# Expert rows scattered straight from the mixer, and expert results added to the token rows in memory by accumulating indirect DMAs

## The reference

```
x = x + xattn(layernorm(x), ctx)          # 16 heads; q and the output projection with int8 fake quantisation
x = x + scan(layernorm(x))                # 16 states per channel, 64 steps, sequential in the tokens
x = x + ffn(layernorm(x))

ffn: probs = softmax(x @ gate_w.T);  scores, idx = top_k(probs, 8)        # 64 experts
     pos = the place of a (token, expert) pair among those of its expert, in token order
     valid = pos < C,  C = 2 * 2048 * 8 / 64 = 512
     xbuf[e, pos] = x[token]  (pairs beyond C are dropped)
     y = (silu(xbuf @ w_gate.T) * (xbuf @ w_up.T)) @ w_down.T
     out[token] += y[e, pos] * score * valid
```

## Time and profile before

| | us |
|---|---|
| median of 3 runs | 2778.35 (2775.64 to 2782.33) |
| the profiled execution | 2786.16 |
| its span in the trace | 2784.4 |
| TensorE busy in the span | 2299.9 (83%) |
| VectorE, ScalarE, GpSimd busy | 1790.8, 1417.8, 976.9 |
| memory traffic | 163.44 MB read, 40.30 MB written |

### The profile page before, as it was taken

The page is one execution under the profiler, slowest core; times in us unless marked ns, Lnnn a source line. Parts: engine busy times, 40 slices in busy tenths (PEclk is TensorE's granted clock), DMA queues, the critical chain, the costliest instruction groups (busy, mean ns, idle before and its releaser), DMA issues. The chain is left out here.

```text
span 2784.4 us, 58439 instructions
## 1 busy us (share of the span) xinstructions
PE 2299.9 (83%) x22156; PEld 1557.6 (56%) x22156; DVE 1790.8 (64%) x3152; ACT 1417.8 (51%) x2948; POOL 976.9 (35%) x1037
## 2 busy tenths in 40 slices
PE   5998999989898989899999999898982399999300
PEld 3665665656565656566565656565651276666200
DVE  4457776877776776777676777777776355454333
ACT  1556565655565565656565656656572144444100
POOL 1112223232323222322322231322223476776576
PEclk9999999999999999999999999999996699999655
DMA  2011101010111111121101010111000388788543
GB/s 78 25 51 54 66 25 63 33 56 33 55 33 56 33 55 38 50 75 37 63 33 55 33 56 33 55 33 56 31 33 36 76 228 223 212 219 210 142 122 111
DMA packets 109499, 207.09 MB, mean 74 GB/s; under 512 B 17136, under 2 KB 86384, under 8 KB 107216
## 3 DMA queue, kind: packets, MB, share of 16 engines
q1 hardware_dynamic: 86688, 153.24, 15.7%
q0 software_dynamic: 22576, 50.56, 8.5%
HBM read 163.44 MB, written 40.30 MB: 73 GB/s over the span
## 5 line engine op out<-in xcount | busy, mean ns | idle before, releaser
L772 ACT ACTIVATE sb_probsT<-W 128x512 f32<-128x512 f32 (+1 forms) x1024 | 472.4, 511 | 420.2 <-PE W L610 418.0
L782 ACT ACTIVATE sb_probs<-S,sb_negmax 128x1604 f32<-128x1604 f32 x256 | 409.1, 1598 | 250.0 <-DVE sb_negmax L939 249.3
L610 PE MATMUL W<-sb_ident,sb_probs 128*128 128x128 f32 (+1 forms) x3328 | 484.8, 284 | 50.5 <-DVE sb_z L1013 50.2
L939 DVE TENSOR_REDUCE sb_negmax<-S 128x1 f32<-128x1604 f32 x256 | 465.7, 1819 | 10.8 <-PE S L600 10.7
L610 PEld LDWEIGHTS W<-sb_ident,sb_probs 128*128 128x128 f32 (+1 forms) x3328 | 357.5, 141 | 167.1 <-issue 104.4
L572 PE MATMUL W<-sb_ctx,sb_wkv_in 128*32 128x401 f32 x4096 | 417.3, 527 | 32.8 <-DVE sb_V L934 27.7
L582 PE MATMUL W<-sb_wkv_in,sb_ctx 128*128 128x256 f32 (+1 forms) x1664 | 422.0, 397 | 21.8 <-DVE sb_K_lo L924 18.9
L625 PE MATMUL O<-sb_probsT,sb_V 128*32 128x128 f32 (+1 forms) x6656 | 331.5, 280 | 41.2 <-ACT sb_probsT L772 39.5
L625 PEld LDWEIGHTS O<-sb_probsT,sb_V 128*32 128x32 f32 (+1 forms) x6656 | 209.3, 110 | 254.7 <-issue 177.8
L582 PEld LDWEIGHTS W<-sb_wkv_in,sb_ctx 128*128 128x128 f32 (+1 forms) x1664 | 301.3, 191 | 82.6 <-DVE sb_K_lo L924 26.0
L924 DVE SCALAR_TENSOR_TENSOR sb_K_lo<-W,sb_pair_cols,sb_K_hi 128x401 fp32r<-128x401 f32 x256 | 161.9, 633 | 281.4 <-ACT sb_K_hi L764 281.4
(11 more groups left out here) (195 smaller groups left out, 3232.4 us busy)
## 6 DMA issues: line engine op xcount, KB each, us to landing
sb_ctx<-ctxT SPq DMA_DIRECT2D x32, 1604.0 KB, 6.6
sb_BC<-bc_scratch SPq DMA_DIRECT2D x16, 2048.0 KB, 7.1
y_scratch<-sb_ys SPq DMA_DIRECT2D x64, 512.0 KB, 4.2
sb_wgu<-wgu SPq DMA_DIRECT2D x64, 192.0 KB, 4.5
sb_wd<-wdT SPq DMA_DIRECT2D x64, 96.0 KB
sb_xg<-ln_scratch,sb_idx POOLq DMA_INDIRECT x256, 5.0
sb_x_q<-x SPq DMA_DIRECT2D x16, 128.0 KB, 2.3
sb_x_res<-x SPq DMA_DIRECT2D x16, 128.0 KB, 2.2
```

Of the source, the lines that this page charges most:

```text
L610: ins = pe.transpose(W[0:keys_in(t), n * P:(n + 1) * P], probs[(slot - 1) % 2][:, t * P:t * P + keys_in(t)], ident[:])
L772: act.activation(probsT[a % 2][0:keys, 0:n], ring[bank_of(i, "T", slot, a)][0:keys, 0:n], ACT.Copy)\
L782: act.activation(probs[slot % 2][:].rearrange("p (c k) -> p c k", c=QUADS), scores_of, ACT.Exp, bias=negmax[:, slot:slot + 1], accum_out=d ...
L939: dve.tensor_reduce(negmax[:, slot:slot + 1], scores_of, AX.XY, ALU.max, negate=True).then_inc(max_done, 1)
```

## The change

Four things change together.

1. Memory holds `xe` (64 * 512 rows of 256, the experts' inputs by slot), `meta` (for each slot a weight and a token number) and two `sums` (2048 rows and 512 spare rows). SP clears `xe` in 32 DMAs of 1 MB, one per slot of the first two rounds, and `meta`, `sums[1]` and the spare rows before them; an empty slot's `meta` is weight 0 and a spare row of its own.
2. `scatter(p)` issues 16 indirect DMAs: for each of the 8 choices the rows of ln3 (1 KB each) into `xe` and (weight, token) (8 bytes) into `meta`. ln3 has its own buffer; x3 is stored to `sums[0]`, and ln3 is not stored. `route` writes `meta` in SBUF and no longer `scores_all` and `slots_all`.
3. In the expert stage SP loads an expert's 512 rows with one DMA of 4 KB pieces (a token's slot is then partition * 4 + c), and all of `meta` with two DMAs in pieces of 32 bytes (`slots`), ahead of expert 1's rows. The copies of Y become multiplications by the slot's weight, two on each engine. GpSimd then adds `ys` to `sums[e % 2]` by four indirect DMAs with `compute_op=ALU.add`. The store to `y` is gone. A buffer of `ys` is free when the four have landed. The experts are unrolled on every engine.
4. The combine adds the two `sums` in four parts of 512 rows and stores them.

```diff
+            def clear(n):
+                rows = E * CAP // CLEARS
+                sp.dma_start(dram["xe"][n * rows:(n + 1) * rows, :].rearrange("(a p c) d -> p a (c d)", p=P, c=4),
+                             none[:].unsqueeze(1).to_broadcast([P, rows // (4 * P), 4 * D])).then_inc(xe_clear, 16)
+            sp.wait_ge(none_up, 2)
+            sp.dma_start(dram["meta"].rearrange("(e p c) o -> p e (c o)", e=E, p=P),
+                         unused[:].rearrange("p c o -> p (c o)").unsqueeze(1).to_broadcast([P, E, 2 * CT])).then_inc(xe_clear, 16)
+            sp.dma_start(dram["sums"][0][TOK:TOK + CAP, :].rearrange("(p c) d -> p (c d)", c=4), none[:]).then_inc(xe_clear, 16)
+            for part in range((TOK + CAP) // CAP):
+                sp.dma_start(dram["sums"][1][part * CAP:(part + 1) * CAP, :].rearrange("(p c) d -> p (c d)", c=4), none[:]).then_inc(xe_clear, 16)
+                    if i * SLOTS + slot < CLEARS:
+                        clear(i * SLOTS + slot)
...
-                        sp.dma_start(dram["x3"][bass.ds((i - 1) * P, P), :], x3[:]).then_inc(x3_out, 16)
-                        sp.dma_start(dram["ln3"][bass.ds((i - 1) * P, P), :], ln3[:]).then_inc(x3_out, 16)
+                        sp.dma_start(dram["sums"][0][(i - 1) * P:i * P, :], x3[:]).then_inc(x3_out, 16)
...
 
             def scatter(p):
 
-                after(pool, scattered, 16 * TOPK * p)
-                pool.tensor_tensor(tokid[:], tokid[:], tile_rows[:], ALU.add).then_inc(tokid_up, 1)
-                pool.wait_ge(tokid_up, 2 * p + 1)
+                if p == 0:
+                    pool.wait_ge(xe_clear, 16 * (CLEARS + 2 + (TOK + CAP) // CAP))
                 pool.wait_ge(dve_up, dve_at(p, "ROUTE"))
-                pool.tensor_tensor(pause_p[:], tile_rows[:], tile_rows[:], ALU.add).then_inc(tokid_up, 1)
+                pool.tensor_tensor(pause_p[:], neg_half[:], neg_half[:], ALU.add).then_inc(idx_seen, 1)
+                pool.wait_ge(idx_seen, p + 1)
                 for t in range(TOPK):
                     pool.indirect_dma_start(
-                        dram["table"], bass.IndirectOffsetOnAxis(ap=sc_idx[:, t:t + 1], axis=0),
-                        tokid[:], None, bounds_check=E * CAP - 1, oob_is_err=False).then_inc(scattered, 16)
+                        dram["xe"], bass.IndirectOffsetOnAxis(ap=sc_idx[:, t:t + 1], axis=0),
+                        ln3[:], None, bounds_check=E * CAP - 1, oob_is_err=False).then_inc(scattered, 16)
+                    pool.indirect_dma_start(
+                        dram["meta"], bass.IndirectOffsetOnAxis(ap=sc_idx[:, t:t + 1], axis=0),
+                        meta[:, t, :], None, bounds_check=E * CAP - 1, oob_is_err=False).then_inc(scattered, 16)
...
+                    after(dve, scattered, 32 * TOPK * p)
...
-                link(dve.tensor_tensor(scores_all[:, bass.ds(p * TOPK, TOPK)], top[:], ok, ALU.mult))
-                link(dve.tensor_scalar(low, pos, float(CAP - 1), None, ALU.min))
-                link(dve.scalar_tensor_tensor(low, idx, float(CAP), low, ALU.mult, ALU.add))
-                link(dve.tensor_copy(slots_all[:, bass.ds(p * TOPK, TOPK)], low))
+                after(dve, scattered, 32 * TOPK * p)
+                link(dve.tensor_tensor(meta[:, :, 0], top[:], ok, ALU.mult))
+                link(dve.tensor_scalar(meta[:, :, 1].bitcast(U32), tokid[:], float(p * P), None, ALU.add))
...
-            sp.dma_start(table[:], dram["table"].rearrange("(e c) o -> e (c o)", e=E)).then_inc(tab_in, 16)
+            def load_x(e, n):
+                after(sp, xt_done, DT * (e - 1))
+                sp.dma_start(xg[n][:], dram["xe"][bass.ds(e * CAP, CAP), :].rearrange("(p c) d -> p c d", p=P)).then_inc(x_in[n], 16)
-            def store(e, n):
-                for m in range(2):
-                    sp.wait_ge(y_up[m], e + 1)
-                sp.dma_start(dram["y"][bass.ds(e * CAP, CAP), :].rearrange("(c p) d -> p c d", p=P), ys[n][:]).then_inc(y_out[n], 16)
+                    load_x(e + 1, 1 - n)
-                if not early(e):
-                    store(e - 2, n)
+            load_x(0, 0)
+            for n, own in enumerate((slice(0, FIRST_SLOTS), slice(FIRST_SLOTS, E))):
+                sp.dma_start(slots[:, own, :, :].rearrange("p e c o -> p e (c o)"),
+                             dram["meta"].rearrange("(e p c) o -> p e (c o)", e=E, p=P)[:, own, :]).then_inc(slots_in[n], 16)
...
-                if not early(e):
-                    pool.wait_ge(x_in[n], in_count(e, n, 16 * CT) - 16 * CT)
-                    pool.wait_ge(xt_done, DT * (e - 1))
-                after(pool, idx_up, 2 * e)
-                pool.tensor_copy(idx[n][:], idx_all[:, bass.ds(e * CT, CT)]).then_inc(idx_up, 1)
-                pool.wait_ge(idx_up, 2 * e + 1)
-                pool.tensor_tensor(pause[:], ident[:, 0:1], ident[:, 0:1], ALU.add).then_inc(idx_up, 1)
+                for m in range(2):
+                    pool.wait_ge(y_up[m], 2 * (e + 1))
+                if e > 1:
+                    pool.wait_ge(y_out[n], in_count(e, n, 16 * CT) - 16 * CT)
-                    pool.indirect_dma_start(xg[n][c][:], None, dram["ln3"],
-                                            bass.IndirectOffsetOnAxis(ap=idx[n][:, c:c + 1], axis=0)).then_inc(x_in[n], 16)
+                    pool.indirect_dma_start(
+                        dram["sums"][n], bass.IndirectOffsetOnAxis(ap=slots[:, e, c, 1:2].bitcast(U32), axis=0),
+                        ys[n][:, c, :], None, bounds_check=TOK + CAP - 1, compute_op=ALU.add).then_inc(y_out[n], 16)
...
-                    after(pe, y_up[m], e)
+                    after(pe, y_up[m], 2 * e)
...
+                act.wait_ge(slots_in[e >= FIRST_SLOTS], 16)
-                    act.wait_ge(y_out[n], (e - n) * 8)
-                act.activation(ys[n][:, 0:2, :], Y[0][:], ACT.Copy).then_inc(y_up[0], 1)
+                    act.wait_ge(y_out[n], (e - n) * 8 * CT)
+                for c in range(2):
+                    act.activation(ys[n][:, c, :], Y[0][:, c, :], ACT.Copy, scale=slots[:, e, c, 0:1]).then_inc(y_up[0], 1)
...
+                dve.wait_ge(slots_in[e >= FIRST_SLOTS], 16)
-                    dve.wait_ge(y_out[n], (e - n) * 8)
-                dve.tensor_copy(ys[n][:, 2:4, :], Y[1][:]).then_inc(y_up[1], 1)
+                    dve.wait_ge(y_out[n], (e - n) * 8 * CT)
+                for c in range(2, CT):
+                    dve.tensor_scalar(ys[n][:, c, :], Y[1][:, c - 2, :], slots[:, e, c, 0:1], None, ALU.mult).then_inc(y_up[1], 1)
...
# combine_phase, new:
+        parts = TOK // CAP
+        one, two = ([ctx.enter_context(nc.sbuf_tensor(f"sb_{m}{n}", [P, CT * D], F32)) for n in range(parts)] for m in ("one", "two"))
+        sum_in = [ctx.enter_context(nc.semaphore(f"sum_in{n}")) for n in range(parts)]
+        sum_up = ctx.enter_context(nc.semaphore("sum_up"))
+        o_out = ctx.enter_context(nc.semaphore("o_out"))
+        def rows(t, n):
+            return t[n * CAP:(n + 1) * CAP, :].rearrange("(p c) d -> p (c d)", p=P)
+            for n in range(parts):
+                sp.dma_start(one[n][:], rows(dram["sums"][0], n)).then_inc(sum_in[n], 16)
+                sp.dma_start(two[n][:], rows(dram["sums"][1], n)).then_inc(sum_in[n], 16)
+            for n in range(parts):
+                sp.wait_ge(sum_up, n + 1)
+                sp.dma_start(rows(out, n), one[n][:]).then_inc(o_out, 16)
+            sp.wait_ge(o_out, 16 * parts)
+            for n in range(parts):
+                dve.wait_ge(sum_in[n], 32)
+                dve.tensor_tensor(one[n][:], one[n][:], two[n][:], ALU.add).then_inc(sum_up, 1)
```

More of the change, by code:

```diff
@@ L262, in mixer_phase @@
         x3 = x2
-        ln3 = ln2
+        ln3 = sb("ln3", [P, D])
+        none = sb("none", [P, 4 * D])
         ln3T = oqT
@@ L1127, in route @@
                 dve.wait_ge(dve_r, p * ROUTE_LINKS + ROUTE_LINKS)
-                after(dve, scattered, 16 * TOPK * p)
                 up(dve.tensor_copy(sc_idx[:], out_))
+            dve.wait_ge(tok_up, 1)
             norm_q(0)
@@ L1184, in expert_phase @@
         ident = sb("ident2", [P, P])
-        pause = sb("pause2", [P, 1])
-        table = sb("table_sb", [E, CAP])
-        idx_all = sb("idx_all", [P, E * CT], U32)
-        idx = [sb(f"idx{n}", [P, CT], U32) for n in range(2)]
-        xg = [[sb(f"xg{n}_{c}", [P, D]) for c in range(CT)] for n in range(2)]
+        xg = [sb(f"xg{n}", [P, CT, D]) for n in range(2)]
+        slots = sb("slots", [P, E, CT, 2])
         wgu = [sb(f"wgu{n}", [P, DT, 2 * FF]) for n in range(2)]
@@ L1221, in expert_phase @@
         y_up = [sem("y_up_act"), sem("y_up_dve")]
+        slots_in = [sem(f"slots_in{n}") for n in range(2)]
         y_out = [sem(f"y_out{n}") for n in range(2)]
@@ L1225, in over_experts @@
         def over_experts(eng, body):
-            for e in range(2):
-                body(e, e)
-            with eng.Fori(1, E // 2 - 1) as two:
-                for n in range(2):
-                    body(2 * two + n, n)
```

(18 more changed lines are left out.)

132 lines of the change are left out of this document (38 added, 94 removed).

## The result

The changed kernel takes **2846.2 us** (median of 4; 2840.5 to 2846.6) where the kernel before takes 2778.6 in the same comparison: 1.0236 times as long over all runs, with a 95% interval of 1.0223 to 1.0249. It is slower by 67.5 us. The forecast was 2719 us, and the range ended at 2820.

What follows compares the result with a forecast made beforehand. TensorE was taken to set the pace in mixer and experts, GpSimd's gathers in the combine. Terms 73 + 20 - 5 + 3 + 8 - 158 = -59 us gave 2727 us profiled, 2719 us as median; range 2655 to 2820.

Steps and rivals of the forecast that it cites:

- Mixer, steady pairs: Mixer, pairs 2 to 15: 16 issues ahead of R2 instead of 8 make TensorE 5.2 us late per pair, +73 us.
- TensorE is late by 6.8 - 1.6 = 5.2: Steady mixer pairs: R2 comes 6.8 us late, less the slack before TensorE's transpose of ln2, leaving 5.2 us per pair.
- Afterwards it is as dense as before: Steady mixer pairs: after its delay TensorE runs as densely as before and catches nothing up, so 14 x 5.2 us.
- the mixer swallows the longer scatter: Rival, mixer: TensorE's 9 us idle per pair absorbs the longer scatter, removing the +73 and giving 2646 us; chance 0.10.
- Mixer, end: Last mixer round and pair 15's scatter: no cover, +9.8 us each and 0.2 for landing, together +20 us.
- Clears: Mixer rounds 0 and 1: SP's 33.5 MB of clears in 32 DMAs run under the mixer and cost nothing.
- Start of the experts: Start of expert stage: one direct load replaces table load and gathers, but 32 B pieces cost 13 us; -5 us.
- Pace of an expert: Expert stage: 6.2 us per expert instead of 6.15, near the limits of ys buffers and DMA engines, +3 us.
- The factor of 1.5 on the issue: Expert stage: upper end of the pace, 7.9 us per expert with four issues at 1.5 times 1.25 us, +110 us.
- the adds are dear: Rival, ys recycling in expert stage: slower than before from a pace of 7.13 us; 2807 us at 7.6; chance 0.25.
- End of the experts: After the last gate product: two scatters of 5.0 us and a landing instead of one 3 us store, +8 us.
- Combine: Last stage: 180.4 us of gathers go, loads, four adds and stores take 22 us instead; -158 us.

Runs made afterwards that it cites:

- e11_seven: Changed kernel with 14 of a pair's 16 scatter issues ahead of R2 and two behind it: 2798.9 us, beside 2775.3 for the kernel before.
- e1_split: Changed kernel with each pair's scatter split, eight indirect DMAs before R2 and eight directly after: 2725.7 us, 0.982 of the kernel before.
- e3_halfrow: Changed kernel with the expert stage's adds on 128 of each row's 256 columns, same number of rows and issues: 2853.4 us.
- e2_plain: Changed kernel with the expert stage's scatters written without the add, so rows overwrite: 2712.2 us.
- e7_two: Changed kernel with two of each expert's four transfers adding and two plain: 2911.8 us, beside 2919.3 for the kernel before.
- e4_fourys: Changed kernel with four buffers of ys and four sums instead of two: 2835.4 us.
- e10_tree: Changed kernel with split scatter, plain scatters to one row per (token, choice), and a tree of adds in the combine: 2630.0 us, 0.948 of before.

## Why the prediction was wrong

**Mixer, steady pairs (predicted +73 for 14 pairs).** The path was right: 16 issues in front of R2, VectorE's wait grown to 7.95 us. R2's lateness was put at 6.8 us and is 7.3 (7.5 on the mean). Two steps failed. The first is the slack in "TensorE is late by 6.8 - 1.6 = 5.2": the transpose began 2.09 us after the start of ln2 and now begins 1.01 after it, so only 1.1 us could be taken off, and the rest is the way from VectorE to TensorE. The second is "Afterwards it is as dense as before": the clock that falls behind the 6 us idle stood nowhere in the sum. Measured against the three pairs of e11_seven with the clock held, the mean period grows by 7.5 (lateness) - 1.2 (slack) + 2.1 (clock, up to z) - 0.9 (fewer falls behind z) = 7.5 us. 13 periods are 97 us; with 5.2 they would have been 68. The fourteenth, from 113.2 to 124.8 us, is longer by 11.6: 7.3 for R2 again, and 4.3 in a stretch in which the granted clock was 0.90 and 0.96 and had been 1.00. In the same pair of e11_seven the clock held, and the way from ln2 to ln3 is 74.4 us, where it is 75.5 before the change and 79.8 after it. Together +108.6. Two readings were off besides. The period of 130.7 us was that of one pair; the pairs of the kernel before alternate between 128.7 and 130.7, and the mean is 129.8. And TensorE's idle pieces are not all "below 1 us each" (us in total, times, longest us):

```profile
PE W L610 <- DVE sb_z L1013: 50.2, 14, 3.6
```

The rival that the mixer swallows the longer scatter falls with the measured +108.6.

**Mixer, end (predicted +20).** The last round is longer by 11.6 (9.6 of it is R2's lateness, 9.8 predicted). From its ln3 to the next stage it is 11.8 more: the last scatter is longer by 10.5 (9.8 predicted), GpSimd's idle behind its last issue by 1.8 (4.72 us, and it was 2.89; predicted 0.2 for the landing), and the scatter starts 0.5 earlier. So +23.4. The start of the mixer gained 2.3 us, perhaps because the table's zeroing is gone. Sum: 108.6 + 23.4 - 2.3 = 129.7.

**Clears (predicted 0).** Right: in e1_split, which has them all, the second ln2 stands at 321.4 us, where it is 323.9 in the kernel before, and the period behind it is unchanged. The row of the clears and that of the adds in the list of DMA issues (count, size, median us to landing); the adds' landing is not the 8 us that the rival needed:

```profile
xe_scratch<-sb_none SPq DMA_DIRECT2D x32, 1024.0 KB, 14.9
...
sum_scratch<-sb_ys,sb_slots POOLq DMA_INDIRECT x256, 4.9
```

**Start of the experts (predicted -5).** To the first hidden product it is 12.4 us instead of 21.9, -9.5. The small pieces did hold SP up, for 5.1 us at the load of expert 1's rows, less than the 13 that one row from the busiest 2 us of the kernel had given:

```profile
2318.51 1.09 SPq L1282 DMA_DIRECT2D sb_slots<-meta_scratch  x2
2319.64 5.06 SPq L1264 DMA_DIRECT2D sb_xg<-xe_scratch  x1
```

**Pace of an expert (predicted 6.15 to 6.2, +3).** This term carries most of the error: 6.12 to 7.37 us, 63 x 1.25 = **+79**. The limits listed were TensorE, the two buffers and the DMA engines, and GpSimd's four issues stood among them only inside the second, at a gather's 1.25 us. The row of the gathers and that of the small scatters agree that an issue does not depend on payload, and I carried that over to another kind of transfer, which no row showed. e3_halfrow confirms the rule for payload, e2_plain and e7_two show that the kind counts. The factor of 1.5 on the issue was named as the end of the range (7.9) and was nearly met (1.57 against 1.00), yet the forecast stood at the cheap end. The rival "the adds are dear" held: it was to decide at 7.13 us of pace or 1.7 us per issue, with the gap, and 1.87 was measured. Its place was wrong, as e4_fourys shows: with buffers to spare the stage is as long.

The Trainium skill's rule ("DMA: Bandwidth & Descriptors", Rules for kernel authors), that an accumulating DMA reads its destination first, was weighed as traffic. The DMA share did rise to 0.91 from 0.81 at fewer GB/s, so the extra work shows; e3_halfrow takes it down to 0.71 and the time does not follow. Here the rule cost nothing, and the price was on the issuing engine.

**End of the experts (predicted +8).** From the last hidden product to the combine it is 30.9 us instead of 8.7, +22. The same cause: GpSimd is behind when TensorE ends, and issues thirteen more adds, one after the other.

**Combine (predicted -158).** -161.2; 19.2 us instead of the 22 worked out.

The sum with the measured terms is 129.6 - 9.5 + 79 + 22 - 161.2 = +59.9, the difference of the spans. Against the forecast the pace is 76 us too long, the mixer 37 and the end of the experts 14, the start of the experts and the combine 8 too short: 119 us, and the other 8 of the 127 between 2719 and 2846 are the step from the profiled execution to the median. The pace alone would have given 2719 - 3 + 77 = 2793 us, inside the range; the mixer and the end of the experts put the time outside it. The adds make some 100 us of the difference to the kernel before, and the scatter's place some 120: e1_split mends the second alone and ends at 0.982 of before, e10_tree mends both and ends at 0.948.

## What to carry to other kernels

Before work is moved onto an engine that issues DMAs, multiply its instructions by their issue time and set the product beside the pace of the loop as a limit of its own; an issue of a kind that the trace does not show is an unknown, even if issues of all sizes cost the same. A longer run of issues can be split around the step that others wait for, and may then cost nothing. Slack in front of a stalled engine counts only without the way between the two engines, and on TensorE a new idle can cost it again through the clock of what follows. Read such a term from many rounds: here the pairs of one kernel differ by up to 5 us, and one pair shown for a theory can speak against the others.
